# Expert stage: rings of six places, buffers reused at a distance of three tiles, one more tile of lead on every engine

## What is computed

```python
x = x + jnp.tanh(g_xattn[0]) * _L0_xattn_ref(_layernorm(x, axis=-1), ctx_1024, ...)
x = x + jnp.tanh(g_ffn[0]) * _L0_ffn_ref(_layernorm(x, axis=-1), ...)
# in _L0_ffn_ref: 8 true experts and 2 null ones, the best two of ten for each of 8192 tokens
gate_probs = jax.nn.softmax(x @ gate_w.T + gate_b, axis=-1)
weights, selected = jax.lax.top_k(gate_probs, TOP_K)
# weights of the true ones, normalized to a sum of 1; then, over the chosen experts e
out = sum_e w_e * (x @ expert_w[e] + expert_b[e])
```

## Time and profile before

| what | value |
|---|---|
| median of 3 runs | 1397.64 us |
| the profiled execution's own time | 1394.18 us |
| its span, first to last instruction | 1392.4 us |
| mean granted TensorE clock | 0.982 |
| TensorE matmuls busy | 1309.5 us, 94% |
| VectorE busy | 1105.9 us, 79% |
| ScalarE busy | 752.4 us, 54% |
| GpSimd busy | 694.2 us, 50% |
| expert stage: first matmul of choice 0 to the last of choice 1 | 974.5 to 1385.5 us |
| DMA, mean over the span | 184 GB/s |

### The profile page before, as it was taken

How to read it: one execution, slowest core, us unless ns; L and a number is a source line. 1 busy time by engine, 2 the same in 40 slices (tenths; PEclk the granted TensorE clock), 3 DMA queues, 4 the chain that set the end, 5 groups by cost and what they waited for, 6 DMA issues and landing times. The chain is left out here.

```text
span 1392.4 us, 30166 instructions
## 1 busy us (share of the span) xinstructions
PE 1309.5 (94%) x7339; PEld 671.3 (48%) x7340; DVE 1105.9 (79%) x2797; ACT 752.4 (54%) x2724; POOL 694.2 (50%) x645
## 2 busy tenths in 40 slices
PE   7999999999999999999999999993998988999997
PEld 5434555555555555555555555541544444444443
DVE  6776888998999999999999999885666665666665
ACT  5655666665666666656656665652443333344332
POOL 1501222445545445445545545545666666666664
PEclk9999999999999999999999999996999999999999
DMA  8144788878977878978779877973455435676772
GB/s 306 50 170 128 184 197 185 192 185 225 213 189 182 188 185 227 218 176 190 190 180 244 205 178 180 185 172 115 134 142 142 146 132 187 220 244 214 229 232 100
DMA packets 413298, 256.17 MB, mean 184 GB/s; under 512 B 338979, under 2 KB 350307, under 8 KB 413077
## 3 DMA queue, kind: packets, MB, share of 16 engines
q1 hardware_dynamic: 385365, 180.89, 53.4%
q0 software_dynamic: 27840, 74.18, 16.8%
HBM read 111.61 MB, written 75.01 MB: 134 GB/s over the span
## 5 line engine op out<-in xcount | busy, mean ns | idle before, releaser
L908 PE MATMUL scores<-arena,zT 128*128 (+2 forms) x2304 | 414.8, 338 | 3.4 <-PEq L159 3.4
L1023 ACT ACTIVATE expd<-scores,less 128x77 f32<-128x77 f32 x1024 | 317.4, 328 | 183.0 <-DVE less L1127 181.9
L923 PE MATMUL mix<-u_sb,pT 128*128 128x512 f16 x1728 | 383.5, 379 | 1.3 <-DMA pT<-p_parts 0.7
L1876 PE MATMUL out_bank<-arena,expert_yT 128*128 x1440 | 334.6, 383 | 5.2 <-issue 3.0
L908 PEld LDWEIGHTS scores<-arena,zT 128*128 128x128 f16 x2304 | 220.6, 98 | 170.0 <-issue 5.7
L923 PEld LDWEIGHTS mix<-u_sb,pT 128*128 128x128 f16 x1728 | 169.0, 98 | 198.3 <-issue 0.8
L1876 PEld LDWEIGHTS out_bank<-arena,expert_yT 128*128 128x128 f16 x1440 | 142.0, 99 | 153.2 <-issue 13.2
L1023 ACT ACTIVATION_READ_ACCUMULATOR expd<-scores,less 128x1 f32 x1024 | 213.4, 208 | 0.0
L1597 POOL DMA_INDIRECT table<-payload,row_i x128 | 159.8, 1248 | 60.1 <-issue 35.8
L1901 ACT CAST expert_yT<-yT_bank 128x512 f16<-128x512 f32 x120 | 70.2, 585 | 211.8 <-PE yT_bank L1863 101.6
L1989 DVE SCALAR_TENSOR_TENSOR result<-out_bank,slots,biased 128x512 f32<-128x512 f32 x120 | 90.1, 751 | 101.3 <-remote 51.5
(11 more groups left out here) (183 smaller groups left out, 1669.6 us busy)
## 6 DMA issues: line engine op xcount, KB each, us to landing
comb<-x_out SPq DMA_DIRECT2D x64, 512.0 KB, 3.2
x_ln<-in_x_dram SPq DMA_DIRECT2D x64, 256.0 KB
x_res<-in_x_dram SPq DMA_DIRECT2D x64, 256.0 KB
w_raw<-in_L_ffn_expert_w_dram SPq DMA_DIRECT2D x64, 128.0 KB, 2.3
u_dram<-u_stage SPq DMA_DIRECT2D x12, 512.0 KB, 2.8
u_sb<-u_dram SPq DMA_DIRECT2D x6, 1024.0 KB, 8.0
arena<-in_L_xattn_w_kv_dram SPq DMA_DIRECT2D x4, 1024.0 KB, 7.9
slots<-table SPq DMA_DIRECT2D x150, 2.0 KB
```

Of the source, the lines that this page charges most:

```text
L908: last = pe.matmul(scores[s][k][:, 0:n], zT[:, s, zp, t, :], m, start=(t == 0 and (zp, mp) == PRODUCTS[0]), stop=(t == DT - 1 and (zp, mp) ...
L923: last = pe.matmul(mix[:], pT[:, s, pp, k, :], u_sb[:, k, up, :], start=(k == 0 and (pp, up) == PRODUCTS[0]), stop=False)
L1023: last = act.activation(expd[:, s, h * KEYS:(h + 1) * KEYS], scores[s][k][:, at:at + KEYS], ACT.Exp, bias=less[:, s, h:h + 1], scale=1.0 / ...
L1876: last = pe.matmul(c.out_bank[s][:], yT[:, s, yp, t, :], w_of[:, bass.ds(e, 1), t, wp * D:(wp + 1) * D].rearrange("p a n -> p (a n)"), sta ...
```

## The change

`RING` goes from 5 to 6, which makes the largest number of passes 12 (from 15) and the list 72 entries long (from 75). `buffer(s)` is `s % TURNS`, so that a turn always comes round after three tiles, and every wait for a free buffer asks for the tile three before. TensorE transposes tile j+2 before it multiplies tile j; ScalarE casts j+2, then normalizes j+3; VectorE takes `low_y(j+2)`, then `name_token(j+6)`, and only then name, bias and finish of j. Gathers go five tiles ahead (`LEAD` = `EARLY` = 5), and the gather of tile j waits for `weigh_bias(j-6)`, the last reading of its place, not for a `finish`. ScalarE's wait for the end of choice 0 becomes waits tile by tile. `expert_yT` and `biased` move into a part of `arena` that is free by then (`spare_room`).

```diff
--- before.py
+++ after.py
@@ -50,7 +50,7 @@
 GROUP = 4
 GROUPS = TILES // GROUP
 RANK0 = 2 * GROUP * GATES
-RING = 5
+RING = 6
 PASSES = -(-(TILES + EXPERTS) // RING)
 LIST = PASSES * RING
 NO_TOKEN = float(TOKENS)
@@ -1664,7 +1664,7 @@
         self.put = [sem(f"put{s}") for s in range(RING)]
 
 
-def run_experts(nc, ident, ones16, w_parts, slots, expert_bias, bias_in, got_rings, comb, x_final, table, listing):
+def run_experts(nc, ident, ones16, w_parts, slots, expert_bias, bias_in, got_rings, comb, x_final, table, listing, spare_room):
 
 
 
@@ -1673,8 +1673,8 @@
 
 
     R = RING
-    EARLY = 4
-    LEAD = 4
+    EARLY = R - 1
+    LEAD = R - 1
 
     TURNS = 3
     with ExitStack() as stack:
@@ -1682,10 +1682,11 @@
             return stack.enter_context(nc.sbuf_tensor(name, shape, dt))
 
         y = sb("expert_y", [P, TURNS, D], F32)
-        biased = sb("biased", [P, TURNS, D], F32)
         result = sb("result", [P, R, D], F32)
-        yT = sb("expert_yT", [P, TURNS, 2, DT, P], F16)
         w_of = w_parts.rearrange("p (e t) x -> p e t x", t=DT)
+        turns = TURNS * 2 * D
+        yT = spare_room[:, 0:turns].rearrange("p (s l t q) -> p s l t q", s=TURNS, l=2, t=DT)
+        biased = spare_room[:, turns:2 * turns].bitcast(F32).rearrange("p (s n) -> p s n", s=TURNS)
         yT_banks = [stack.enter_context(nc.psum_tensor(f"yT_bank{s}", [P, DT, P], F32)) for s in range(TURNS)]
         out_banks = [stack.enter_context(nc.psum_tensor(f"out_bank{s}", [P, D], F32)) for s in range(TURNS)]
         one_ring, two_ring = got_rings
@@ -1725,7 +1726,7 @@
 
         def buffer(s):
 
-            return s % R % TURNS
+            return s % TURNS
 
         def experts(engine, c, r):
 
@@ -1807,7 +1808,7 @@
                 pool.wait_ge(c.token_ready, (j - EARLY if c.k == 1 else j) + 1)
                 if later(j, R):
 
-                    pool.wait_ge(c.result_ready, 2 * (j - R) + 2)
+                    pool.wait_ge(c.biased_ready, j - R + 1)
                 pool.nop(nofuse=True)
                 if c.k == 0:
                     gather(c.got[s], one_ring[:, s], halves, c.token[:, s, :])
@@ -1857,8 +1858,8 @@
 
             def transpose_y(c, j, s):
                 pe.wait_ge(c.y_ready, j + 1)
-                if later(j, 2):
-                    pe.wait_ge(c.y_lo_ready, j - 1)
+                if later(j, TURNS):
+                    pe.wait_ge(c.y_lo_ready, j - TURNS + 1)
                 for t in range(DT):
                     last = pe.transpose(c.yT_bank[s][:, t, :], y[:, s, t * P:(t + 1) * P], ident[:])
                 last.then_inc(c.yT_summed, 1)
@@ -1866,11 +1867,11 @@
             def multiply(c, j, s, e, first_tiles):
                 pe.wait_ge(c.y_hi_ready, j + 1)
                 pe.wait_ge(c.y_lo_ready, j + 1)
-                if later(j, 2):
-                    pe.wait_ge(c.result_ready, 2 * (j - 1))
+                if later(j, TURNS):
+                    pe.wait_ge(c.result_ready, 2 * (j - TURNS + 1))
                 elif c.k == 1:
 
-                    pe.wait_ge(choices[0].result_ready, 2 * (first_tiles - 1 + j))
+                    pe.wait_ge(choices[0].result_ready, 2 * (first_tiles - TURNS + 1 + j))
                 for t in range(DT):
                     for yp, wp in PRODUCTS:
                         last = pe.matmul(c.out_bank[s][:], yT[:, s, yp, t, :],
@@ -1882,28 +1883,32 @@
             tiles = None
             for c in choices:
                 def step(r, s, live, pass_experts):
-                    if live(1):
-                        transpose_y(c, R * r + s + 1, buffer(s + 1))
+                    if live(2):
+                        transpose_y(c, R * r + s + 2, buffer(s + 2))
                     if live(0):
                         multiply(c, R * r + s, buffer(s), pass_experts[s], tiles)
 
                 if c.k == 1:
                     pe.wait_ge(listing.listed, 2)
-                tiles = run(pe, c, step, 1, uses_experts=True)
+                tiles = run(pe, c, step, 2, uses_experts=True)
 
         @block.scalar
         def _(act):
-            def high_y(c, j, s):
+            def high_y(c, j, s, first_tiles):
                 act.wait_ge(c.yT_summed, j + 1)
-                if later(j, 2):
-
-                    act.wait_ge(c.expert_summed, j - 1)
+                if later(j, TURNS):
+
+                    act.wait_ge(c.expert_summed, j - TURNS + 1)
+                elif c.k == 1:
+                    act.wait_ge(choices[0].expert_summed, first_tiles - TURNS + 1 + j)
                 act.copy(yT[:, s, 0], c.yT_bank[s][:]).then_inc(c.y_hi_ready, 1)
 
-            def normalize(c, r, s, j):
+            def normalize(c, r, s, j, first_tiles):
                 act.wait_ge(c.got[s], 16 * r + 16)
-                if later(j, 2):
-                    act.wait_ge(c.yT_summed, j - 1)
+                if later(j, TURNS):
+                    act.wait_ge(c.yT_summed, j - TURNS + 1)
+                elif c.k == 1:
+                    act.wait_ge(choices[0].yT_summed, first_tiles - TURNS + 1 + j)
                 act.nop(nofuse=True)
                 own = slots[:, c.k, bass.ds(j, 1), 2:4].rearrange("p a b -> p (a b)")
                 act.activation(y[:, buffer(s), :], c.x_got[:, s, :], ACT.Identity, bias=own[:, 0:1],
@@ -1913,21 +1918,17 @@
                 act.activation(ring, ones16[:, 0:1].broadcast_to([P, n]), ACT.Copy, scale=0.0).then_inc(cleared, 1)
 
             clear(one_ring[:].rearrange("p s d -> p (s d)"), R * D)
+            tiles = None
             for c in choices:
                 def step(r, s, live, _):
-                    if live(1):
-                        high_y(c, R * r + s + 1, buffer(s + 1))
                     if live(2):
-                        normalize(c, *at(r, s, 2))
+                        high_y(c, R * r + s + 2, buffer(s + 2), tiles)
+                    if live(3):
+                        normalize(c, *at(r, s, 3), tiles)
                     if c.k == 0 and first_pass(r) and s >= 0:
                         clear(two_ring[:, s].rearrange("p l d -> p (l d)"), 2 * D)
 
-                if c.k == 1:
-
-                    act.wait_ge(choices[0].yT_summed, tiles)
-                    act.wait_ge(choices[0].expert_summed, tiles)
-                    act.nop(nofuse=True)
-                tiles = run(act, c, step, 2)
+                tiles = run(act, c, step, 3)
 
         @block.vector
         def _(dve):
@@ -1949,8 +1950,8 @@
 
             def low_y(c, j, s):
                 dve.wait_ge(c.y_hi_ready, j + 1)
-                if later(j, 2):
-                    dve.wait_ge(c.expert_summed, j - 1)
+                if later(j, TURNS):
+                    dve.wait_ge(c.expert_summed, j - TURNS + 1)
                 dve.tensor_tensor(yT[:, s, 1], c.yT_bank[s][:], yT[:, s, 0], ALU.subtract).then_inc(c.y_lo_ready, 1)
 
             def weigh_bias(c, r, s, j, e):
@@ -1958,8 +1959,8 @@
                 own = slots[:, c.k, bass.ds(j, 1), 0:2].rearrange("p a b -> p (a b)")
                 if c.k == 1 and isinstance(j, int) and j < EARLY:
                     dve.wait_ge(early_sum_in[s], 16)
-                if later(j, 2):
-                    dve.wait_ge(c.result_ready, 2 * (j - 1))
+                if later(j, TURNS):
+                    dve.wait_ge(c.result_ready, 2 * (j - TURNS + 1))
                     dve.nop(nofuse=True)
                 dve.scalar_tensor_tensor(biased[:, buffer(s), :],
                                          expert_bias[:, bass.ds(e, 1), :].rearrange("p a n -> p (a n)"), own[:, 1:2],
@@ -1997,16 +1998,16 @@
             tiles = None
             for c in choices:
                 def step(r, s, live, pass_experts):
-                    if live(1):
-                        low_y(c, R * r + s + 1, buffer(s + 1))
+                    if live(2):
+                        low_y(c, R * r + s + 2, buffer(s + 2))
+                    named = R if c.k == 0 else EARLY
+                    if live(R) and not (first_pass(r) and s + R < named):
+                        name_token(c, *at(r, s, R))
                     if live(0):
                         j = R * r + s
                         name_out(c, r, s, j, tiles)
                         weigh_bias(c, r, s, j, pass_experts[s])
                         finish(c, r, s, j)
-                    named = R if c.k == 0 else EARLY
-                    if live(R) and not (first_pass(r) and s + R < named):
-                        name_token(c, *at(r, s, R))
                     if c.k == 0 and first_pass(r) and s == 3:
                         dve.wait_ge(*entries(1, 0))
                         for early in range(EARLY):
@@ -2053,7 +2054,7 @@
         slots = stack.enter_context(nc.sbuf_tensor("slots", [P, TOP_K, LIST, 4], F32))
         got_rings = [stack.enter_context(nc.sbuf_tensor("one_ring", [P, RING, D], F32)),
                      stack.enter_context(nc.sbuf_tensor("two_ring", [P, RING, 2, D], F32))]
```

(2 more changed lines are left out.)

## The result

The changed kernel takes 1422.3 us (median of four runs, 1421.3 to 1425.0), the kernel before 1397.8 beside it: ratio 1.0182 [1.0165, 1.0199], +24.5 us, where +12.95 was forecast and 1419 was the top of the range. The profiled execution took 1423.04 us, with a span of 1421.2; before it was 1394.18 and 1392.4. So the two profiles differ by 28.8 us.

A forecast was written before the change was run, and what follows sets the result against it. TensorE was taken as the bound, its idle time the possible gain. 18.2 + 1.4 - 4.5 - 0.65 - 3.3 + 0.5 + 1.3 = +12.95 us on 1397.64 gave 1410.6 us, range 1391 to 1419.

The forecast's parts named there:

- More tiles, +18.2: TensorE: passes of six round 120 tiles up to 126; six more at 3.027 us each cost +18.2 us.
- Rival C: The tile count does not grow as worked out (choice 0 at 48 tiles): 1391.1 us, chance 0.04.
- Lead for transposes, -4.5 and -0.65: TensorE: a spare tile of yT ends 5 late multiplies, -4.5 us, and a bank hold by low_y in tile 46, -0.65.
- Late transposes, 0: TensorE behind ScalarE's late casts: queue order is unchanged, so the 25.4 us of idle time stay, change 0.
- Gathers earlier, -3.3: Choice 1: gathers issued further ahead, after weigh_bias, make the 7 late ones vanish, -3.3 us.
- the terms that I put at nothing: List length, SyncE fetches, moved tensors, name_token ahead of bias and finish: 0 us; VectorE has 56 us spare in choice 0.
- First full gather, +1.3: Choice 1: first gather by token waits behind five gathers of sums, not four, holding back transposes: +1.3 us.
- The run-ups: Start: TensorE transposes three tiles before its first multiply, +0.5 us; at the passage that multiply stays where it is, 0.
- Rival B: Nothing comes back: late multiplies and gathers turn into late transposes, +21.4 us, 1419.0 us, chance 0.12.

The follow-up runs named there:

- e3: The changed kernel with one inner pass fewer in each choice, 114 tiles instead of 126, three real tiles left out: 1386.7 us, ratio 0.9913.
- e11: The kernel before with passes and rings of six and the change's earlier gathers, but distances of two tiles: 1424.6 us, ratio 1.0198.
- e9: The changed kernel itself, unaltered, run again on the chip of e10 and e11: 1425.1 us, ratio 1.0195 to the kernel before.
- e10: The kernel before with only the change's earlier gathers and VectorE's earlier name_token; passes of five, distances of two: 1403.3 us, ratio 1.0043.
- e6: The changed kernel with EARLY = 4, so four tiles of choice 1 instead of five are gathered ahead of choice 0's end: 1422.4 us.
- e1: The changed kernel with ScalarE's order exchanged, normalize of tile j+3 before the cast of tile j+2: 1409.9 us, ratio 1.0076.
- e8: e1 with tile 4 of choice 1 cast ahead of the wait for the first full gather: 1403.4 us, ratio 1.0102 to the kernel before.
- e2: The kernel before with ScalarE's order exchanged, normalize of tile j+2 before the cast of tile j+1: 1397.6 us, ratio 0.9987.
- e13: The changed kernel with a forced pause every second tile, TensorE waiting for its transposes' word before the multiply: 1423.0 us, ratio 1.0170.
- e7: e1 with one more TensorE wait: transposes j+2 issue only once transposes j+1 have reported: 1406.5 us, ratio 1.0115 to the kernel before.
- e17: The changed kernel with the forced TensorE pause of e13 in every third tile in place of every second: ratio 1.0159 to the kernel before.
- e5: The kernel before with passes and rings of six and five gathers ahead, but distances of two and late gathers kept: 1406.9 us, ratio 1.0142.

## Why the prediction was wrong

- **More tiles, +18.2:** right. 1512 matmuls, 54 and 72 tiles, a beat of 3.02, 2.97 us a tile in e3. Rival C, that the count might not grow, is out.
- **Lead for transposes, -4.5 and -0.65:** the multiplies are on time as predicted (4.3 to 0.6 us), but the gain did not reach the end. e11 against e9 puts the distances at 0 within 4 us, where the sum had -5.15.
- **Late transposes, 0:** the step that failed. I had read the chain rightly (transposes, cast, normalize, transposes, in the same order on both queues), and took what it costs as given: 25.4 us, and 1.4 for the new tiles. It isn't given. In the changed kernel it struck as often as before (25 stalls for 24), but for 30.3 us in place of 21.4 by brackets; in e10 it struck 28 times for 35.3 us. All idle time before transposes went from 30.2 to 41.2 us. Words are prompt for two tiles after a stall and late from the third on in more than half of the cases, so a stall that is taken away can come back as another. Why they are late, and why the stalls grew longer, stays open.
- **Gathers earlier, -3.3:** the normalizes no longer wait, as predicted, but the part alone cost 6.0 us (e10). In choice 1 of its profile the idle time stayed (23.0 and 23.3 us) with the late gathers gone: one stall for another. In choice 0, where no gather had delayed TensorE, it rose from 15.9 to 23.8, with a stall every third tile. The order of `name_token` was among the terms that I put at nothing, as VectorE had time to spare. Why the new order of VectorE's `name_token` or the gathers' new times bring that is open; e10 doesn't part the two.
- **First full gather, +1.3:** 4.8 against 3.6 us, right in size, but not by the fifth `early_sum` (e6). The run-ups were small, as said. The half-clock multiplies, +4.7 in the profile, had no term.

18.2 for the tiles, 6.0 for the gathers and 0 for the distances are 24.2 of the measured 24.5; that they meet so closely is in part luck, as the last two are known to some 2.4 and 4 us. Rival B ("nothing comes back", 1419.0) was nearest, and its reason too: one stall replaces another. It was 3.3 us short; e10 says that the earlier gathers didn't only gain nothing, but cost. The Trainium skill (Perfetto Trace Analysis, Optimization Strategy) says that a repeating gap on the saturated engine can mean too few buffers. A distance of three alone left the gap (e9 against e11). Together with ScalarE's exchanged order the idle time before transposes and multiplies was 31.6 us (e1) and 21.3 (e8) in place of 40.1 (e9), each on another chip, and at a distance of two that order gave nothing (e2). So the rule alone didn't help here, and whether the distance does once the order is changed is left open by the gathers, which differ between e1 and e2.

## What to carry to other kernels

Count what a rounding adds before anything else: six empty tiles were three quarters of this result. Where an engine's idle time follows words that come late, the stalls are not a list from which one can be struck: expect the next one to take its place. Before a longer distance, look for what waits for the late word, on any queue, ahead of what is needed next; here the distance alone gave nothing. And before a late instruction is put down to a late word, look at what the instruction ahead of it on its engine waited for (e1).

## What the hardware showed that I had not expected

- Words of finished TensorE work come up to 3 us late in a pattern: seldom for two tiles after a stall (27 of 537), then in 141 of 242 third tiles. Many come close to the end of the multiply behind them: 23 of 37 late casts in e10, 17 of 37 in the changed kernel and 12 of 32 before start within 0.3 us of it, most of the others earlier. Then the word of a multiply and that of the transposes behind it can come together (1004.04 in e10). Pauses every second tile brought late casts from 38 to 9 of 126 (e9, e13). The cause is open: for sequencer run-ahead by over one multiply nothing speaks (e7), one word came 2 us late with the array idle (e13), and half of the words straight behind a pause were late in e17.
- A wait of TensorE for its own last matmul costs 0.52 us of its beat (3.55 us in place of 3.03, e13), while a cast on ScalarE starts 0.04 us after the same transposes' end.
- At the jump into the last pass of choice 0 TensorE stood idle for 3.1 us in the changed kernel, waiting for nothing that the profile shows. Before, multiplies 45 and 46, at the same place, came 2.0 and 1.4 us late, so the jump is hardly a part of the difference.
- The kernel before took 1388.9 us on one chip and 1397.4 to 1398.6 on the others, while e6 took 1422.4 there, as the changed kernel elsewhere. So a ratio doesn't take the chip out either, and differences of a half per cent need both kernels on one chip. The ratios of e5 to e8 are to be read with that in mind.
